# A gated attention unit on one core: rotation by one table product and a fold, repeated products of resident weights between TensorE's steps, scores moved to a shared bank

## The reference

```python
x = _ln(x, ln1_w, ln1_b)
qk = _silu(x @ Wqk.T + bqk)                      # 32 wide
v = _silu(x @ Wv.T + bv)                         # 256 wide
heads = qk[..., None, :] * gamma + beta          # four heads of 32
quad_q, lin_q, quad_k, lin_k = (heads[..., i, :] for i in range(4))
quad_q, lin_q, quad_k, lin_k = map(_rope, (...)) # rotation: x1*cos - x2*sin, x2*cos + x1*sin
...
# within groups of 64 tokens: relu(quad_q quad_k^T / 64 + bias(distance))**2 @ v
# over all tokens:            lin_q @ (lin_k^T @ v) / 256
# times the gate silu(x @ Wg.T + bg), projected by Wo, _ln again, added to x
```

## Time and profile before

| | |
|---|---|
| time before, median of 3 runs | 2129.3 us (2128.28 to 2129.81) |
| profiled execution, first to last instruction | span 2134.5 us |
| its own time | not listed apart from the span |
| TensorE busy, mean granted clock | 1807.3 us (85%), 0.890 |
| VectorE, ScalarE, GpSimd busy | 1259.6, 688.6, 585.9 us |
| the gated unit | about 340 to 594 us of the span |

### The profile page before, as it was taken

The page is one execution under the profiler, slowest core; times in us unless marked ns, Lnnn a source line. Parts: engine busy times, 40 slices in busy tenths (PEclk is TensorE's granted clock), DMA queues, the critical chain, the costliest instruction groups (busy, mean ns, idle before and its releaser), DMA issues.

```text
span 2134.5 us, 38192 instructions
## 1 busy us (share of the span) xinstructions
PE 1807.3 (85%) x10652; PEld 1360.9 (64%) x10653; DVE 1259.6 (59%) x4249; ACT 688.6 (32%) x1279; POOL 585.9 (27%) x946
## 2 busy tenths in 40 slices
PE   3759993888834599479999979999999998999998
PEld 2548991444433499468888855555555555988997
DVE  2546884666544588656656645655655652656654
ACT  0115550222200255223223214444444443223222
POOL 2653775555247366631221010000000000000000
PEclk9658996787755699789999979999999999999999
DMA  5111212000001122200000000000000000000001
GB/s 196 39 45 50 61 49 92 21 18 19 5 20 43 57 58 60 57 23 11 14 15 10 1 1 1 1 1 0 0 0 0 0 0 1 1 0 0 0 1 40
DMA packets 61674, 54.01 MB, mean 25 GB/s; under 512 B 8467, under 2 KB 54932, under 8 KB 61077
## 3 DMA queue, kind: packets, MB, share of 16 engines
q1 hardware_dynamic: 51958, 34.11, 5.2%
q0 software_dynamic: 8192, 16.79, 2.6%
q10 hardware_dynamic: 1440, 2.10, 0.3%
HBM read 31.48 MB, written 21.50 MB: 25 GB/s over the span
## 4 chain that ended last, share of the span: by engine, by line
PE 70%; issue 10%; DVE 9%; POOL 6%; DMA 2%; SPq 1%; ACT 1%; POOLq 1%; DVEq 1%; ACTq 0%
PE bk L1007 14%; PE bk L1656 10%; PE bk L582 6%; PE bk L990 5%; PE bk L992 5%; PE bk L991 5%; PE bk L1644 3%; PE bk L575 3%; PE bk L1631 2%; PE bk L1582 2%; PE bk L564 2%; PE bk L566 2%; PE bk L565 2%; DMA sb_X<-x 1%; POOL sb_xf L455 1%
## 5 line engine op out<-in xcount | busy, mean ns | idle before, releaser
L1007 PEld LDWEIGHTS bk<-sb_wd,sb_sc 128*128 128x128 f32 (+1 forms) x2688 | 332.9, 191 | 24.8 <-DVE sb_X L1106 3.6
L1007 PE MATMUL bk<-sb_wd,sb_sc 128*128 128x128 f32 (+1 forms) x2688 | 336.9, 275 | 0.9 <-issue 0.8
L1092 DVE TENSOR_TENSOR sb_sc<-sb_sb_,bk 128x512 f32<-128x512 f32 x224 | 152.2, 684 | 240.5 <-PE bk L992 190.4
L112 POOL TENSOR_TENSOR sb_ln_ve<-sb_ln_mv,sb_eps 128x2 f32<-128x2 f32 (+1 forms) x48 | 9.4, 195 | 1010.2 <-DVE sb_ln_mv L104 1010.2
L1046 ACT ACTIVATE sb_sb_<-bk 128x512 f32<-128x512 f32 x224 | 133.9, 598 | 450.8 <-PE bk L992 448.4
L1910 DVE TENSOR_REDUCE sb_sc<-bk 128x2 f32<-128x512 f32 x256 | 164.6, 687 | 156.2 <-PE bk L1631 152.1
L1656 PE MATMUL bk<-sb_sa,sb_sb_ 128*32 128x256 f32 x1024 | 247.4, 385 | 0.7 <-ACT sb_sc L1805 0.7
L1818 ACT ACTIVATE sb_sa<-bk 128x512 f32<-128x512 f32 x256 | 151.1, 597 | 182.8 <-PE bk L1644 182.8
L1106 DVE SCALAR_TENSOR_TENSOR sb_X<-bk,sb_gate,sb_X 128x128 f32 (+1 forms) x576 | 161.4, 342 | 4.2 <-PE bk L1007 1.8
L582 PE MATMUL bk<-sb_w2c,sb_sb_ 128*128 x1152 | 152.1, 275 | 0.0
L368 POOL DMA_INDIRECT xs<-sb_xn,sb_send_row x128 | 128.8, 1006 | 83.6 <-DVE sb_send_row L357 48.3
(11 more groups left out here) (279 smaller groups left out, 3418.7 us busy)
## 6 DMA issues: line engine op xcount, KB each, us to landing
sb_sc<-xs SPq DMA_DIRECT2D x144, 64.0 KB, 1.8
ys<-sb_sc SPq DMA_DIRECT2D x36, 256.0 KB, 2.3
xs<-sb_xn,sb_send_row POOLq DMA_INDIRECT x128
out<-sb_X SPq DMA_DIRECT2D x1, 2048.0 KB, 8.7
sb_sa<-w SPq DMA_DIRECT2D x1, 1792.0 KB, 13.3
sb_sc<-w SPq DMA_DIRECT2D x1, 1792.0 KB, 17.8
sb_sa<-w_gu SPq DMA_DIRECT2D x1, 1760.0 KB
xs<-sb_zeros SPq DMA_DIRECT2D x24, 64.0 KB, 17.8
```

What stands on the lines that cost most here:

```text
L1007: ins = pe.matmul(bank[:, j * P:(j + 1) * P], p.hT[0:m, c % HRING, j * P:(j + 1) * P], p.wd[0:m, q * D:(q + 1) * D], start=(c == FIRST[e] ...
L1092: dve.tensor_tensor(p.hT[0:m, c % HRING, :], p.sg[0:m, c % 2, :], p.bk[2 + c % 2][0:m, :], ALU.mult)\
```

## The change

Four things, all in the gated unit:

1. **Rotation.** The projection of the heads gives 128 rows in place of 64: the 64 of before and the same with the halves of each head swapped (the weights hold both). A table `ga_rt` of gamma times cosine (rows 0 to 63) and gamma times sine (rows 64 to 127) is multiplied in one VectorE instruction over 128 partitions; a product with a 128x64 matrix of zeros and ones (`ga_fold`) adds both halves; a second VectorE instruction adds the rotated beta (`ga_rb`). Two instructions take the place of five.
2. **Repeated products.** `ga_warm_pe` issues products of `w1h` with itself, 256 columns, into bank 5, whose result nothing reads: two in front of the scores, behind the scores, behind the key transposes, in front of the output transposes and in front of the key-value product.
3. **Bank.** The scores go to the upper half of bank 4, whose lower half holds the key-value product. That product now also waits for VectorE to have read the scores.
4. **Tables.** `ga_rt` and `ga_rb` are made once, in the preparation of the weights.

```diff
-    pe.matmul(p.bk[0][0:NQ, S:2 * S], p.ga_w[:, 0:NQ], p.ga_xa[:], start=True, stop=True).then_inc(p.ga_qkp.sem, 1)
+    pe.matmul(p.bk[0][:, S:2 * S], p.ga_w[:, 0:2 * NQ], p.ga_xa[:], start=True, stop=True).then_inc(p.ga_qkp.sem, 1)
...
-def ga_swap_pe(pe, p, b):
-
-    pe.wait_ge(p.ga_hd.sem, p.ga_hd.at(2 * b + 2))
+def ga_fold_pe(pe, p, b):
+
+    pe.wait_ge(p.ga_hd.sem, p.ga_hd.at(b + 1))
     pe.sem_inc(p.pe_passed.sem, 1)
-    pe.matmul(p.bk[3][0:NQ, :], p.ga_perm[:], flat(p.ga_h[:]), start=True, stop=True).then_inc(p.ga_sw.sem, 1)
+    pe.matmul(p.bk[3][0:NQ, :], p.ga_fold[:], flat(p.ga_h[:]), start=True, stop=True).then_inc(p.ga_sw.sem, 1)
...
+def ga_warm_pe(pe, p, n):
+
+    for _ in range(n):
+        pe.matmul(p.bk[5][:, 0:S], p.w1h[:, 0:P], p.w1h[:, 0:S], start=True, stop=True)
...
     rp, vg = p.ga_r[:, par], p.ga_v[:, par]
-    pe.wait_ge(p.ga_rp.sem, p.ga_rp.at(3 * b + 3))
+    ga_warm_pe(pe, p, 2)
+    pe.wait_ge(p.ga_rp.sem, p.ga_rp.at(b + 1))
     pe.wait_ge(p.ga_at.sem, p.ga_at.at(2 * b))
     for t in range(NB2):
         c = slice(t * P, (t + 1) * P)
-        ins = pe.matmul(p.bk[5][:, c], rp[0:QK, 1, c], rp[0:QK, 0, c], start=True, stop=True)
+        ins = pe.matmul(p.bk[4][:, S + t * P:S + (t + 1) * P], rp[0:QK, 1, c], rp[0:QK, 0, c], start=True, stop=True)
     ins.then_inc(p.ga_scp.sem, 1)
+    ga_warm_pe(pe, p, 2)
     pe.wait_ge(p.ga_o.sem, p.ga_o.at(b))
...
     ins.then_inc(p.ga_lkp.sem, 1)
+    ga_warm_pe(pe, p, 2)
     if not last:
         ga_x_pe(pe, p, b + 1)
     if behind:
+        ga_warm_pe(pe, p, 2)
         ga_turn_out_pe(pe, p, b - 1)
+    ga_warm_pe(pe, p, 2)
     pe.wait_ge(p.ga_lk.sem, p.ga_lk.at(b + 1))
     pe.wait_ge(p.ga_kv.sem, p.ga_kv.at(b))
+    pe.wait_ge(p.ga_at.sem, p.ga_at.at(2 * b + 1))
     pe.wait_ge(p.ga_vg.sem, p.ga_vg.at(NB2 * b + NB2))
...
-    for n in range(2):
-        dve.tensor_scalar(p.ga_h[:, n, :], p.ga_q[:], p.ga_gb[:, 2 * n:2 * n + 1], p.ga_gb[:, 2 * n + 1:2 * n + 2],
-                          ALU.mult, ALU.add).then_inc(p.ga_hd.sem, 1)
...
-    dve.tensor_tensor(p.ga_r1[:], p.ga_h[:], by_position(p.ga_cos), ALU.mult).then_inc(p.ga_rp.sem, 1)
...
+    dve.tensor_tensor(p.ga_h[:], p.ga_q[:].unsqueeze(1).to_broadcast([P, 2, S]), p.ga_rt[:], ALU.mult)\
+       .then_inc(p.ga_hd.sem, 1)
+
+
+def ga_turned_dve(dve, p, b, par):
 
     dve.wait_ge(p.ga_sw.sem, p.ga_sw.at(b + 1))
-    dve.tensor_tensor(p.ga_r2[:], p.bk[3][0:NQ, :].rearrange("p (a s) -> p a s", a=2), by_position(p.ga_sin), ALU.mult)\
+    dve.tensor_tensor(p.ga_r[:, par], p.bk[3][0:NQ, :].rearrange("p (a s) -> p a s", a=2), p.ga_rb[:], ALU.add)\
        .then_inc(p.ga_rp.sem, 1)
-    dve.wait_ge(p.ga_rp.sem, p.ga_rp.at(3 * b + 2))
-    dve.tensor_tensor(p.ga_r[:, par], p.ga_r1[:], p.ga_r2[:], ALU.add).then_inc(p.ga_rp.sem, 1)
...
+    pe.wait_ge(p.gar.sem, p.gar.at(4))
+    pe.matmul(p.bk[3][0:NQ, :], p.ga_fold[:], flat(p.ga_h[:]), start=True, stop=True).then_inc(p.gar.sem, 1)
     pe.wait_ge(p.gaw.sem, p.gaw.at(6))
+    pe.wait_ge(p.gar.sem, p.gar.at(6))
...
+    for n in range(2):
+        dve.tensor_scalar(p.ga_h[:, n, :], p.ga_trig[:], p.ga_gb[:, 2 * n + 1:2 * n + 2], None, ALU.mult)\
+           .then_inc(p.gar.sem, 1)
+        dve.tensor_scalar(p.ga_rt[:, n, :], p.ga_trig[:], p.ga_gb[:, 2 * n:2 * n + 1], None, ALU.mult)\
+           .then_inc(p.gar.sem, 1)
+    dve.wait_ge(p.gar.sem, p.gar.at(5))
+    dve.tensor_copy(flat(p.ga_rb[:]), p.bk[3][0:NQ, :]).then_inc(p.gar.sem, 1)
```

More of the change, by code:

```diff
@@ L1270, in ga_pe_element @@
     if not last:
-        ga_swap_pe(pe, p, b + 1)
+        ga_fold_pe(pe, p, b + 1)
     pe.wait_ge(p.ga_at.sem, p.ga_at.at(2 * b + 2))
@@ L1283, in ga_pe @@
     ga_project_pe(pe, p, 0)
-    ga_swap_pe(pe, p, 0)
+    ga_fold_pe(pe, p, 0)
     ga_pe_element(pe, p, 0, 0, behind=False)
@@ L1303, in ga_silu_act @@
     act.wait_ge(p.ga_qkp.sem, p.ga_qkp.at(b + 1))
-    act.wait_ge(p.ga_hd.sem, p.ga_hd.at(2 * b))
-    act.activation(p.ga_q[:], p.bk[0][0:NQ, S:2 * S], ACT.Silu).then_inc(p.ga_qk.sem, 1)
+    act.wait_ge(p.ga_hd.sem, p.ga_hd.at(b))
+    act.activation(p.ga_q[:], p.bk[0][:, S:2 * S], ACT.Silu).then_inc(p.ga_qk.sem, 1)
     if not isinstance(b, int) or b >= 1:
@@ L1404, in ga_dve_element @@
     dve.wait_ge(p.ga_scp.sem, p.ga_scp.at(b + 1))
-    dve.scalar_tensor_tensor(out=p.ga_a1, in0=p.bk[5][:, 0:S].rearrange("p (t k) -> p t k", t=NB2),
+    dve.scalar_tensor_tensor(out=p.ga_a1, in0=p.bk[4][:, S:2 * S].rearrange("p (t k) -> p t k", t=NB2),
                              scalar=1.0 / GROUP, in1=p.ga_bias[:].unsqueeze(1).to_broadcast([P, NB2, P]),
@@ L1421, in ga_dve_element @@
     if not last:
-        ga_sin_dve(dve, p, b + 1, 1 - par)
+        ga_turned_dve(dve, p, b + 1, 1 - par)
     dve.wait_ge(p.ga_op.sem, p.ga_op.at(b + 1))
@@ L1445, in ga_dve @@
     ga_heads_dve(dve, p, 0)
-    ga_cos_dve(dve, p, 0)
-    ga_sin_dve(dve, p, 0, 0)
+    ga_turned_dve(dve, p, 0, 0)
     ln_apply(dve, p, 1, p.xn[:, 0], P - 1, NB2, True)
@@ L1502, in ga_weights_pe @@
     pe.wait_ge(p.dma_ga.sem, p.dma_ga.at(p.nga))
-    for n, c in enumerate((slice(0, NQ), slice(NQ, NQ + 2 * H))):
+    for n, c in enumerate((slice(0, 2 * NQ), slice(2 * NQ, NW))):
         out = p.bk[n][:, 0:c.stop - c.start]
@@ L2124, in work_space @@
     at = Space(t.sb_)
-    w.update(ga_xa=at.take(P, S), ga_q=at.take(NQ, S), ga_h=at.take(NQ, 2, S), ga_r1=at.take(NQ, 2, S),
-             ga_r2=at.take(NQ, 2, S), ga_r=at.take(NQ, 2, 2, S), ga_k=at.take(P, P), ga_s=at.take(NQ, H))
+    w.update(ga_xa=at.take(P, S), ga_q=at.take(P, S), ga_h=at.take(P, 2, S), ga_r=at.take(NQ, 2, 2, S), ga_k=at.take(P, P), ga_s=at.take(NQ, H))
     at = Space(t.sc)
@@ L2352, in gated_unit_layout @@
     qk = f["Wqk"].T
-    w = np.concatenate([qk, qk, f["Wv"].T, f["Wg"].T], 1)
+    half = QK // 2
+    turn = (np.arange(QK) + half) % QK
+    w = np.concatenate([qk, qk, qk[:, turn], qk[:, turn], f["Wv"].T, f["Wg"].T], 1)
     ln_b = np.zeros((P, P), np.float32)
@@ L2358, in gated_unit_layout @@
     ga, be = f["gamma"], f["beta"]
-    half = QK // 2
     freq = (10000.0 ** (-np.arange(half, dtype=np.float32) / half)).astype(np.float32)
@@ L2362, in gated_unit_layout, with by_row @@
     sin, cos = np.sin(angle).T.astype(np.float32), np.cos(angle).T.astype(np.float32)
-    perm = np.zeros((NQ, NQ), np.float32)
-    for i in range(NQ):
-        perm[i // QK * QK + (i + half) % QK, i] = 1
     i = np.arange(P)
+    fold = (i[:, None] % NQ == np.arange(NQ)[None]).astype(np.float32)
+    def by_row(a):
+        return np.concatenate([a[0], a[1], a[0][turn], a[1][turn]])
     same = (i[:, None] // GROUP) == (i[None] // GROUP)
@@ L2373, in gated_unit_layout @@
         ga_raw=w, ga_last=w[P - 1:P], ga_ln_w=f["ln1_w"].reshape(P, 1), ga_ln_w_last=f["ln1_w"].reshape(P, 1)[P - 1:P],
-        ga_ln_b=ln_b, ga_brow=np.concatenate([f["bqk"], f["bqk"], f["bv"], f["bg"]])[None], e_last=e_last,
-        ga_gb=np.stack([np.concatenate([ga[0], ga[1]]), np.concatenate([be[0], be[1]]),
-                        np.concatenate([ga[2], ga[3]]), np.concatenate([be[2], be[3]])], 1),
-        ga_cos=np.concatenate([cos] * 4, 0), ga_sin=np.concatenate([-sin, sin] * 2, 0), ga_perm=perm,
+        ga_ln_b=ln_b, ga_brow=np.concatenate([f["bqk"], f["bqk"], f["bqk"][turn], f["bqk"][turn], f["bv"], f["bg"]])[None], e_last=e_last,
+        ga_gb=np.stack([by_row(ga[0:2]), by_row(be[0:2]), by_row(ga[2:4]), by_row(be[2:4])], 1),
+        ga_trig=np.concatenate([cos] * 4 + [-sin, sin] * 2, 0), ga_fold=fold,
         ga_wo=f["Wo"].T.reshape(2, P, D).transpose(1, 0, 2).reshape(P, 2 * D), ga_bo=f["bo"][None],
```

27 lines of the change are left out of this document (11 added, 16 removed).

## The result

The changed kernel takes 2112.5 us (median of 4 runs, 2112.31 to 2114.72) against 2129.6 us of the kernel before on the same chip: ratio 0.9923, 95% interval 0.9909 to 0.9937, 17 us less. The forecast was 2121.

The account below looks back on a forecast made before the run. GpSimd's waits for VectorE were taken to bound the pairs, TensorE close behind. Four pairs give 6.0 us, the next 1.8, the last elements 1.3, preparation takes 0.5: 8.6 off 2129.3, 2121 us, range 2109 to 2134.

Parts of the forecast that it names:

- GpSimd's ring: GpSimd's ordered gathers, powers and bias with its waits for VectorE: sets a pair of elements, 27.7 to 26.2 us.
- Heads: VectorE in front of the statistics: three instructions become one, 0.76 us saved, twice a pair of elements.
- TensorE's ring: TensorE from gate through moments, output transposes and output to the next gate: 25.5 us a pair, 2 to spare.
- Sum behind the fold: Two VectorE instructions behind the fold become one, 0.68 us less, hidden by other waits, so worth 0.
- Repeated products, 0.13 each: Ten an element on TensorE, 0.26 us for two at full clock; four of five places hidden in waits.
- Bank's wait: Key-value product waits until VectorE has read the scores: 0.45 us an element more on TensorE.
- Clock: one fall an element: TensorE's clock in the gated unit still falls but returns sooner: costs 1.3 us an element instead of 1.67.
- the first rival: Products close the pauses and TensorE's clock never falls: 17.2 us less, 2112 us; chance 0.20.
- Preparation, 0.5 us: Making the tables before the first gathered rows are added: 4.9 us of work under 5.3 of cover, 0.5 charged.
- the tail: Elements behind the last gather: four of 13.63 us go to 13.3, 1.3 us gained.
- The slower rival: Products and the key-value product's wait delay TensorE 0.95 us an element, clock no better: 2134 us; chance 0.19.
- nothing to be seen: GpSimd's work gets shorter, TensorE's takes over near 27.5 us a pair, clock as now: 2127 to 2131 us; chance 0.15.

Follow-up runs that it names:

- the second pair of edits: Changed kernel with VectorE's heads ahead of the residual and two short float32 transposes in place of each repeated product: 2109.4 us, ratio 0.9911.

## Why the prediction was right, and where not

The direction was right and the time lies in the range, but the forecast has half of the gain: 8.6 us, where 17.0 were measured. The range of 2109 to 2134 takes in the times of all three rivals, so lying in it says little for the sum. Of the signs that were named, most were seen: one heads instruction of 0.69 us, pairs of 26.0 to 26.3, the residual's wait behind GpSimd (3.27 us in the element shown, from 1.11 up in others), the key-value product right behind L1404. The clock was seen above the forecast.

- *GpSimd's ring binds the pairs, 26.2 us after the change.* Right: 26.0 to 26.3, and one instruction more in it, twice a pair, costs 1.1 a pair.
- *Heads, 0.76 us twice a pair.* Right: GpSimd's wait went from 3.08 to 2.33 us.
- *TensorE's ring is 25.5 with 2 us to spare.* Wrong: this was read in a pair at a mean clock of 0.82. With the rotation alone the clock is 0.76 and the ring takes 27.3. A ring whose work depends on the clock has no length apart from the clock that it gets.
- *Sum behind the fold, worth 0.* Not borne out: doubling it costs 3.4 us by the medians, which is at the edge of the noise. Whether taking it out gained anything no run shows.
- *Repeated products, 0.13 each.* The product was right (0.12), the term was not: a place costs 0.19 on top, 0.43 a pair in place of 0.26. In the pairs it does not show, since GpSimd's ring binds them. Behind the last gather it does: there the chain runs through the products. Of the Trainium skill (TensorE: Matmul & The Clock Gate, Back-to-back issue gap), from which the prediction took 109 ns for such a product when warm, the trace's 0.12 for one more is a tenth over; the 0.19 is not in it.
- *Bank's wait, 0.45 us an element on TensorE's ring.* The wait is there, the cost is not seen (0.3 us between two kernels that differ by it, in its favour), though not where it would hold up a ring that binds. Nor did the fifth pair of products show as a cost: leaving it out gained nothing.
- *Clock: one fall an element, 1.3 us.* This is the step that failed. The choice between 0 and 1.67 was put near the upper end because the products fill only half of the waiting time. TensorE was at half for 33 us in place of 103, and in three of the five pairs not at all (1.00). Over the window from 404 to 534, ten elements at a mean clock of 0.95, that is 13 us at half, which is a loss of at most 0.65 us an element in place of 1.3; where the clock stayed at 1.00 it is the first rival's 0. In the pairs this changed nothing, since GpSimd's ring binds them at 26.2 with either figure; it counts behind the last gather.
- *Preparation, 0.5 us.* Hidden: the adding of the first group comes 0.7 us later than before, and the phase itself began 1.0 later.
- *Sum.* Five pairs 8.5 (forecast 7.8), the pair ahead 2.9 (put at nothing, without a reason), the tail 4.1 (1.3). The last two are together 7.0 in place of 1.3: 5.7 of the 8.5 us that the forecast lacks, and in both stretches the clock rose. The tail's gain is the products' (4.8 with them alone, 0.2 with the rotation alone). That of the pair ahead needs both: the products alone raise its clock from 0.73 to 0.81 (window from 379 to 404 us) and it takes 27.3 us, the rotation alone 26.3, both 23.8. Why is not shown.
- The rival "the clock stays at full", chance 0.20, gave 2112, which is nearest in time, and in part by luck: three of the five pairs are as it said, but its tail is not (8.5 forecast, 4.1 seen), and the pair ahead makes up for some of that (1 forecast, 2.9 seen). The clock of 0.86 in the tail is not all of the reason: with four products a place it is 1.00 from 534 to 565 us and the tail 45.2, with transposes 44.5, which is 5.0 and 5.7 less than before and not 8.5. The reckoning also left out that the products are on the chain there:

```profile
541.71 0.43 PE bk L1244 x2
...
562.35 0.43 PE bk L1244 x2
...
564.11 1.16 PE bk L1244 x4
```

These are rows of the chain behind the last gather, profile after; with three more places the products are 3.3 us of it.

- The slower rival needed products on the path with the clock no better; "nothing to be seen" is what the rotation alone does, 0.9984.

Open: the runs are 17 us apart and the phase is 15.7 shorter; the other 1.3 were not traced. Why transposes hold the clock better than fewer, longer products do was not settled; the place they fill is also longer (0.59 against 0.43). What holds the clock in one pair and lets it fall in the next (1.00 and 0.87 by turns in the changed kernel) was not found either.

## What to carry to other kernels

Where two engines' rings are within a few per cent of each other, an edit of one tells little about its worth: look for the edit of the other that must go with it, and test the pair (3.5 and 5.2 us alone, 16.3 together; for the second pair of edits, close to the noise, 0.8 and 1.5 lost alone, 3 won together). Before giving an engine some spare time, ask at which clock that time was read. And to keep TensorE's clock in a loop full of short waits, spare work in each wait can pay, as long as another ring binds; where TensorE's own does, as behind the last gather here, part of the work is on the path (it still won 4.8 us there). Count the place as well as the instruction.

## What was not expected of the hardware

- Float32 transposes of resident data in the pauses held the granted clock at 1.00 through all pairs (12 us at half in all), as four products a place did. By the Trainium skill (TensorE: Matmul & The Clock Gate, Part 4: PE-mode transpose) the full clock doesn't engage for transposes, since they don't count as a busy engine in the same way. This kernel's runs don't agree: transposes alone in the pauses keep a clock that falls without them (12 us at half against 114). Whether transposes alone would raise it no run here shows, as products stand between them.
- A short run of float32r products of 128 by 256 between float32 products takes 0.19 us plus 0.12 for each, from its start to the next instruction.
- Less work for VectorE went with a lower clock for TensorE: the window from 456 to 482 us has 0.83 before and 0.76 with the rotation alone, though its pairs got shorter (27.5 to 28.4 us before, 27.3 to 27.4 after). The cause was not shown.
